# Sorted expert blocks: both ranks from one product, expert numbers read seven at a time, batch 0 joined from block 24

## The reference, cut to what matters

```python
x = x + L0_gnn(layernorm(x), adj)          # 8 batches of 1024 rows, 128 features
x = x + L0_ffn(layernorm(x))               # the part the change touches
x = x + L1_gnn(layernorm(x), adj)
x = x + L1_ffn(layernorm(x))

def L0_ffn(x):                             # 8 experts, the best 2 for each row
    xn = normalised x * gamma + beta
    logits = xn @ Wr + br
    top_vals, top_idx = top_k(logits, 2)
    w = softmax(top_vals)
    y_e = gelu(xn @ W1[e] + b1[e]) @ W2[e] + b2[e]      # 128 -> 256 -> 128
    return sum of the two chosen y_e, weighted with w
```

## Time and profile before

| | before |
|---|---|
| median of 3 runs | 1110.0 us |
| the profiled execution, its own time | 1111.47 us |
| its span in the trace | 1109.7 us |
| mean granted TensorE clock | 0.985 |
| PE busy | 1028.6 us (93%) |
| DVE busy | 687.6 us (62%) |
| ACT busy | 767.0 us (69%) |
| POOL busy | 383.1 us (35%) |

### The profile page before, as it was taken

How to read it: one execution, slowest core, us unless ns; L and a number is a source line. 1 busy time by engine, 2 the same in 40 slices (tenths; PEclk the granted TensorE clock), 3 DMA queues, 4 the chain that set the end, 5 groups by cost and what they waited for, 6 DMA issues and landing times. The chain is left out here.

```text
span 1109.7 us, 20072 instructions
## 1 busy us (share of the span) xinstructions
PE 1028.6 (93%) x6446; PEld 743.4 (67%) x6446; DVE 687.6 (62%) x2171; ACT 767.0 (69%) x1176; POOL 383.1 (35%) x468
## 2 busy tenths in 40 slices
PE   4798789788899998799999999999999999999998
PEld 3466556465476777478888888886466666666667
DVE  5678898768654347388999899762533333333336
ACT  4998899776564555488888888885656556556561
POOL 4123778878573222556565653201000000000000
PEclk9999999999899999899999999999999999999999
DMA  8967987723237664423333322110000000000001
GB/s 301 342 268 270 392 318 277 279 72 124 70 97 249 189 196 140 125 68 86 87 91 90 92 84 73 60 30 1 1 10 10 10 20 10 10 19 11 10 16 33
DMA packets 70730, 128.53 MB, mean 116 GB/s; under 512 B 10094, under 2 KB 36316, under 8 KB 69596
## 3 DMA queue, kind: packets, MB, share of 16 engines
q1 hardware_dynamic: 61852, 109.34, 29.1%
q0 software_dynamic: 8192, 16.79, 5.0%
q10 hardware_dynamic: 576, 1.05, 0.3%
HBM read 76.69 MB, written 50.46 MB: 115 GB/s over the span
## 5 line engine op out<-in xcount | busy, mean ns | idle before, releaser
L2428 PEld LDWEIGHTS eY<-Vo,dGW 128*128 128x128 f32 x1024 | 132.5, 192 | 54.0 <-issue 52.7
L588 POOL DMA_INDIRECT sorted_x<-V,AT_I x128 | 125.2, 978 | 58.7 <-issue 37.2
L2428 PE MATMUL eY<-Vo,dGW 128*128 128x128 f32 x1024 | 134.2, 276 | 0.1
L2598 DVE TENSOR_TENSOR dGW<-H,WBC 128x512 f32<-128x512 f32 x80 | 55.3, 692 | 124.9 <-PE eY L2428 124.8
L2411 PE MATMUL eU<-XTN,V 128*128 128x512 f32 x256 | 131.0, 594 | 0.9 <-PEq L2346 0.9
L777 PE MATMUL O<-Y,HS 128*128 128x512 f32 x256 | 131.4, 634 | 0.0
L2419 PE MATMUL eU<-H,V 128*128 128x512 f32 x256 | 131.1, 594 | 0.0
L2029 POOL DMA_INDIRECT W<-sorted_y,ROW_I x96 | 96.8, 1009 | 70.2 <-PE f_T L2103 50.3
L2507 ACT ACTIVATE H<-eU,bn 128x512 f32<-128x512 f32 x128 | 99.5, 777 | 25.5 <-PE eU L2411 16.2
L2130 PEld LDWEIGHTS f_O<-f_XN,f_PT 128*128 128x128 f32 x896 | 106.8, 192 | 12.8 <-DVE X L2241 10.4
L2130 PE MATMUL f_O<-f_XN,f_PT 128*128 128x128 f32 x896 | 109.8, 276 | 2.7 <-DVE X L2241 2.0
(11 more groups left out here) (328 smaller groups left out, 2074.6 us busy)
## 6 DMA issues: line engine op xcount, KB each, us to landing
XTN<-in_adj SPq DMA_DIRECT2D x64, 512.0 KB, 7.3
masks<-NMW SPq DMA_DIRECT2D x8, 2048.0 KB
f_MK<-masks SPq DMA_DIRECT2D x60, 256.0 KB, 2.8
sorted_y<-zero SPq DMA_DIRECT2D x36, 256.0 KB
NMW<-sorted_x SPq DMA_DIRECT2D x25, 256.0 KB, 2.8
sorted_y<-NMW SPq DMA_DIRECT2D x25, 256.0 KB
X<-in_x SPq DMA_DIRECT2D x8, 512.0 KB, 8.3
out_x<-X SPq DMA_DIRECT2D x16, 256.0 KB, 2.3
```

Source lines behind the costliest of these rows:

```text
L588: g_.indirect_dma_start(sorted_x, bass.IndirectOffsetOnAxis(ap=AT_I[b % 2][:, kt:kt + 1], axis=0), XR[b % 2][:, t * P:(t + 1) * P], None). ...
L2428: i = pe.matmul(Y[q][:, t * P:(t + 1) * P], GW[:, j % 2, t * P:(t + 1) * P], Vo[:, e * P:(e + 1) * P], start=(e == 0 and t == 0), stop=(e ...
L2598: v.tensor_tensor(GW[:, j % 2, :], h2(j), WBC[:, e, q * HALF:(q + 1) * HALF], ALU.mult).then_inc(gw_ready, 1)
```

## The change

It does four things. `rank_wholes` and `take_wholes` go: `used_blocks` now also counts each place's blocks less twice those taken early (`filled[:, 1]`), and one product of two columns gives both ranks, next to the count of blocks below (`rank_blocks`, in step 4). `take_rest` (step 4) then makes the wholes and the parts, with two more small instructions; `list_blocks` and `list_rest` move to step 5 and `list_stores` to step 6. DVE's `expert` reads one number at a time for blocks up to 24 and seven at a time for blocks 25, 32 and 39. POOL's gathers of batch 0 wait for `turned >= 18 + t // 2`. JOIN, NORM and TURN each come three blocks earlier.

```diff
-        TAKEN, TO_READY, UNTIL_READY = 5, 12, 13
+        TAKEN, TO_READY, UNTIL_READY = 5, 10, 11
...
-            JOIN, NORM, TURN, LATE, ROWS_STEP = 27, 38, 40, 17, 2 * E + 1
+            JOIN, NORM, TURN, LATE, ROWS_STEP = 24, 35, 37, 17, 2 * E + 1
...
-                    pool.wait_ge(turned, 18 + t)
+                    pool.wait_ge(turned, 18 + t // 2)
...
-                def rank_wholes():
-                    pe.wait_ge(table_step, TAKEN + 1)
-                    pe.matmul(TB[:, 0:1], before[:, :], ubf[:, :], start=True, stop=True).then_inc(table_step, 1)
-
                 def rank_blocks():
-                    pe.wait_ge(table_step, TAKEN + 3)
-                    pe.matmul(TB[:, 0:1], before[:, :], ubf[:, :], start=True, stop=True)
-                    pe.matmul(TB[:, 1:1 + E], ones[:, :], below[:, :], start=True, stop=True).then_inc(table_step, 1)
+                    pe.wait_ge(table_step, TAKEN + 1)
+                    pe.matmul(TB[:, E:E + 2], before[:, :], ubf[:, :], start=True, stop=True)
+                    pe.matmul(TB[:, 0:E], ones[:, :], below[:, :], start=True, stop=True).then_inc(table_step, 1)
...
                     if k == 4:
-                        rank_wholes()
+                        rank_blocks()
                     if k == 5:
-                        rank_blocks()
-                    if k == 6:
                         list_blocks()
...
-                    v.tensor_copy(ubf[:, :], filled[:, :]).then_inc(table_step, 1)
                     op(v.tensor_tensor, used[:, :], used2[:, 0:1], used2[:, 1:2], ALU.add)
-                    v.tensor_scalar(below[:, :], upto[:, :], used[:, :], None, ALU.mult)
+                    op(v.scalar_tensor_tensor, out=filled[:, 1:2], in0=taken[:, :], scalar=-2.0, in1=used[:, :],
+                       op0=ALU.mult, op1=ALU.add)
+                    v.tensor_copy(ubf[:, :], filled[:, :])
+                    v.tensor_scalar(below[:, :], upto[:, :], used[:, :], None, ALU.mult).then_inc(table_step, 1)
...
-                    v.tensor_copy(ubf[:, :], both[:, :]).then_inc(table_step, 1)
-
-                def take_rest():
-                    dve.wait_ge(table_step, TAKEN + 4)
-                    op(v.tensor_copy, got[:, :], TB[:, 0:1])
-                    op(v.tensor_tensor, pick8[:, :], mine[:, :], TB[:, 1:1 + E], ALU.mult)
+                    op(v.tensor_scalar, places[:, 0:1], places[:, 0:1], float(WHOLES - EARLY), -2.0, ALU.min, ALU.mult)
+                    op(v.tensor_tensor, got[:, :], places[:, 0:1], places[:, 1:2], ALU.add)
+                    op(v.tensor_tensor, pick8[:, :], mine[:, :], TB[:, 0:E], ALU.mult)
...
                 def expert(k):
-                    return dve.value_load(EXPERT[0:1, k:k + 1], min_val=0, max_val=E - 1)
+                    if k < WHOLES:
+                        return dve.value_load(EXPERT[0:1, k:k + 1], min_val=0, max_val=E - 1)
+                    if (k - WHOLES) % 7 == 0:
+                        _, seven = nc.values_load_multi_w_load_instructions(EXPERT[0:1, k:k + 7], engines=[mybir.EngineType.DVE],
+                                                                            min_val=0, max_val=E - 1)
+                        for i in range(7):
+                            experts[k + i] = seven[i]
+                    return experts.pop(k)
...
                     if k == 4:
-                        take_wholes()
+                        take_rest()
                     if k == 5:
-                        take_rest()
+                        list_rest()
                     if k == 6:
-                        list_rest()
-                    if k == 7:
                         list_stores()
```

More of the change, by code:

```diff
@@ L313, in program @@
             pf, ef, used, got, rel = (tile(n, [P, 1]) for n in ("pf", "ef", "used", "got", "rel"))
-            ubf, below = tile("ubf", [P, 1], BF16), tile("below", [P, E], BF16)
+            ubf, below = tile("ubf", [P, 2], BF16), tile("below", [P, E], BF16)
             taken, rest, both = tile("taken", [P, 1]), tile("rest", [P, 2]), tile("both", [P, 1])
+            places = tile("places", [P, 2])
             used2, part_rows, hot2 = tile("used2", [P, 2]), tile("part_rows", [P, 1]), tile("hot2", [P, NR])
-            filled, later, least = tile("filled", [P, 1]), tile("later", [P, 1]), tile("least", [1, 4])
+            filled, later, least = tile("filled", [P, 2]), tile("later", [P, 1]), tile("least", [1, 4])
             within, upto_k = tile("within", [P, 2]), tile("upto_k", [1, 2])
@@ L388, in program @@
             X0_MEANS, X0_ROOT, X0_NORM, X0_TURNED, X0_READ = 1, 3, 5, 7, 9
-            JOIN, NORM, TURN, LATE, ROWS_STEP = 27, 38, 40, 17, 2 * E + 1
+            JOIN, NORM, TURN, LATE, ROWS_STEP = 24, 35, 37, 17, 2 * E + 1
             OTHERS, ROWS_FROM = RING + 1, RING + 1
-            assert HC == 2 and NB == 46 and NT == 8 and ROWS_FROM + E < 18 and WHOLES == 25 and EARLY + 16 - 4 <= 24 < JOIN and RING + E // 2 == EARLY == RING + 4
+            assert HC == 2 and NB == 46 and NT == 8 and ROWS_FROM + E < 18 and WHOLES == 25 and EARLY + 16 - 4 <= 24 <= JOIN and RING + E // 2 == EARLY == RING + 4
             assert JOIN + NT + 1 < NORM and TURN + 3 < NB
@@ L818, in _ @@
                         pe.wait_ge(table_step, 1)
-                        pe.matmul(M[1][:, 0:1], before[:, :], ubf[:, :], start=True, stop=True).then_inc(table_step, 1)
+                        pe.matmul(M[1][:, 0:1], before[:, :], ubf[:, 0:1], start=True, stop=True).then_inc(table_step, 1)
                     if b == LAST and c == 2:
@@ L826, in _ @@
                         route(b - 1, range(4, NT))
-                TB, TC, PL = M[0][:, 0:1 + E], M[1][:, 0:5 * NB + 4], M[1][:, HALF - P:HALF]
+                TB, TC, PL = M[0][:, 0:2 + E], M[1][:, 0:5 * NB + 4], M[1][:, HALF - P:HALF]
                 def turn(k):
@@ L1253, in full_blocks @@
                     op(v.tensor_tensor, full[:, :], got[:, :], rowno[:, :], ALU.is_ge)
-                    v.tensor_copy(ubf[:, :], full[:, :]).then_inc(table_step, 1)
+                    v.tensor_copy(ubf[:, 0:1], full[:, :]).then_inc(table_step, 1)
                 def take_full():
@@ L1277, in used_blocks, with take_rest @@
                     op(v.tensor_scalar, got[:, :], got[:, :], -float(WHOLE - PART), None, ALU.add)
-                    op(v.tensor_tensor, filled[:, :], got[:, :], rowno[:, :], ALU.is_ge)
-                    op(v.tensor_tensor, filled[:, :], filled[:, :], taken[:, :], ALU.subtract)
-                    v.tensor_copy(ubf[:, :], filled[:, :]).then_inc(table_step, 1)
+                    op(v.tensor_tensor, filled[:, 0:1], got[:, :], rowno[:, :], ALU.is_ge)
+                    op(v.tensor_tensor, filled[:, 0:1], filled[:, 0:1], taken[:, :], ALU.subtract)
                     op(v.tensor_tensor, used[:, :], used2[:, 0:1], used2[:, 1:2], ALU.add)
-                    v.tensor_scalar(below[:, :], upto[:, :], used[:, :], None, ALU.mult)
-                def take_wholes():
+                    op(v.scalar_tensor_tensor, out=filled[:, 1:2], in0=taken[:, :], scalar=-2.0, in1=used[:, :],
+                       op0=ALU.mult, op1=ALU.add)
+                    v.tensor_copy(ubf[:, :], filled[:, :])
+                    v.tensor_scalar(below[:, :], upto[:, :], used[:, :], None, ALU.mult).then_inc(table_step, 1)
+                def take_rest():
                     dve.wait_ge(table_step, TAKEN + 2)
-                    op(v.tensor_copy, got[:, :], TB[:, 0:1])
-                    op(v.tensor_scalar, hot[:, EARLY:WHOLES], kth[:, 0:WHOLES - EARLY], got[:, :], filled[:, :], ALU.is_equal, ALU.mult)
+                    op(v.tensor_copy, places[:, :], TB[:, E:E + 2])
+                    op(v.tensor_scalar, hot[:, EARLY:WHOLES], kth[:, 0:WHOLES - EARLY], places[:, 0:1], filled[:, 0:1], ALU.is_equal,
+                       ALU.mult)
                     op(v.tensor_reduce, later[:, :], hot[:, EARLY:WHOLES], AX_X, ALU.add)
@@ L1303, in take_rest @@
                     v.tensor_tensor(hot[:, WHOLES:NB], hot[:, WHOLES:NB], hot2[:, :], ALU.add).then_inc(table_step, 1)
-                    op(v.tensor_scalar, pick8[:, :], TB[:, 1:1 + E], float(PART), -float(SPARE), ALU.mult, ALU.add)
+                    op(v.tensor_scalar, pick8[:, :], TB[:, 0:E], float(PART), -float(SPARE), ALU.mult, ALU.add)
                     v.scalar_tensor_tensor(out=shift8[:, :], in0=order[:, :], scalar=float(SEATS), in1=pick8[:, :],
```

11 lines of the change are left out of this document (5 added, 6 removed).

## The result

| | before | changed |
|---|---|---|
| median, 20 runs each | 1109.51 us | 1111.58 us |
| lowest to highest | 1107.19 to 1112.18 | 1110.39 to 1115.04 |
| time changed / before | | 1.0020, 95% interval 1.0012 to 1.0027 |
| the profiled execution, its own time | 1111.47 us | 1111.38 us |
| its span in the trace | 1109.7 us | 1109.6 us |

The changed kernel takes 2.07 us more, 0.2%. That is small, but the interval leaves no change out.

The account below looks back on a forecast made before the run. PE bounds the loop, waiting in blocks 7 to 15 for loads held behind table TO, and in 256-row blocks for weights DVE copies. A -2.4 plus B +3.2 gives +0.8: 1110.8 us on the median, range 1107.5 to 1113.4.

Parts of the forecast that it names:

- Part B: Blocks of 256 rows, work(24) to work(45): early join and bulk reads together cost +3.2 us, bounds +0.8 to +5.0.
- The table one step earlier: Before block 7: TO ends 2.7 us earlier, PE is 0.7 us behind at work(7), loads of rows come sooner.
- 0.6 us of waits that were to stay: At the load of block 16: PE still waits 0.4 us, plus 0.2 for SP's reads that may be slowed.
- A: Table's part, work(4) to work(24): of 3.7 us lost, 0.7 lost at the table, 0.6 stay: -2.4, bounds -3.0 to -1.5.
- Joining from step 24: First join on DVE: gathers have landed by 400, DVE comes at about 402; waiting on them costs nothing.
- The joins' own waits: Join steps on PE: 0.1 us lost in each of five, 0.6 once behind a 512-row finish; 1.1 in all.
- Seven numbers a read: DVE's reads for blocks 25, 32, 39: 1.5 us each plus register work; PE stalls 1.0, 3.5 and 1.5 us.
- the prediction's own signs: Wrong if bulk read lasts well under 1 us or over 2, no block 32 stop, or SP waits at 12 or 13.
- the norm's wait: In the 256-row blocks: 0.3 us of old waits at the norm go with the new order.
- the cheap read: Rival, chance 0.18: seven numbers cost 0.67 us like three, B is +0.8, time 1107.8 or less, faster.
- The dear read: Rival, chance 0.16: seven numbers take 2.1 us or more, B +5.0, sum +2.6, 1112.6 us; decides from about 2.0.
- The table that buys nothing: Rival, chance 0.06: SP waits at block 12 or 13 for rows POOL sends, A about -0.5, 1112.7 us.

Follow-up runs that it names:

- x3: The kernel before with the bulk reads of seven alone, without the early table or the early join: 1115.09 us, 1.0046 of before.
- x4: The kernel before with the early join alone (join from block 24, gathers less held back): 1110.15 us, 1.0003 of before.
- x6: x5 with the late join again (blocks 27, 38 and 40, gathers one per block): 1105.09 us, 0.9968 of before.
- x10: The changed kernel with the late join again, so early table and reads of seven remain: 1111.32 us against 1109.38, 1.0029 of before.
- x1: The changed kernel with expert numbers read one at a time again; early table and early join stay: 1105.88 us, 0.9966 of before.
- x2: The kernel before with the table one step earlier and nothing else: 1107.27 us, 0.9975 of before.
- x5: The changed kernel with the 21 expert numbers read ahead, three at a time, in block steps 17 to 23: 1104.52 us against 1109.66, 0.9965.
- x7: The changed kernel with three numbers to a read instead of seven, still read where the first is wanted: 1110.51 us, 1.0013 of before.
- x8: x5 with the 21 numbers read ahead seven at a time, in block steps 17, 19 and 21: 1108.25 us, 0.9995 of before.

## Why the prediction was right, and where it wasn't

The forecast, within 0.2% of before at 1110.8 us, held by a hair: 1111.58 us lies in the range, and +2.07 us (+1.3 to +3.0) stands at the edge of what was called the same. The mechanism was the predicted one: the table gains about 3 us, and the bulk reads stop PE at three places and cost more than that. The total is in part luck. Part B, +5.80 us, lies outside its own bounds (+0.8 to +5.0), 2.6 us above the sum; the table gained 0.5 us more than the sum had it, near its best bound; and the medians differ by +2.07 where the loop of the profiles is +2.9.

- **The table one step earlier: right, step by step.** With the 3.55 us added, the trace has `work(5)` at 320.37 (predicted 320.45), `hot` done at 324.68 (324.65), `work(6)` at 325.41 (325.4), `work(7)` at 329.46 (329.4), TO at 326.85 (326.9) and the load of block 16 at 360.01 (360.15). Only the 0.6 us of waits that were to stay did not: A is -2.89 against -2.4. Against the other executions of the same code (x3, x4) it is -1.8 and -2.2, so the 2.4 was as good as the spread allows.
- **Joining from step 24: right.** The waits for gathers cost nothing, and x4, x6 and x10 show that the early join moves the time by nothing measurable. The joins' own waits were 0.6 + 0.15 + 0.15 us, predicted 1.1. Two of the eight joins, not three, meet longer steps of PE (in x1, steps 24 and 25 last 3.72 and 2.87 us).
- **Seven numbers a read: right in kind and place, too small.** The three stops stand at blocks 25, 32 and 39 as predicted, at 1.35, 3.00 and 2.52 us (6.9) instead of 1.0, 3.5 and 1.5 (6.0). The term that was mis-sized is "0.30 + 6 x 0.20 = 1.5 us": it took one duration for all three, while the read takes 2.15, 1.07 and 2.09. By the prediction's own signs, a read of over 2 us counts against it, and two of the three are. Where the read took 1.07 the stop was 0.5 us shorter than predicted, where it took 2.1 it was 0.35 and 1.0 us longer. At block 39 the read explains only some 0.3 of the 1.0: with its register work it is 2.09 + 7 x 0.27 = 4.0 us, where the prediction had 1.5 + 7 x 0.31 = 3.7. The other 0.7 us is cover that the sum put too high there. The 0.31 us a number for register work and hand-over came out at some 0.27: block 39's read ends at 433.0 + 2.09 = 435.1, and the last of its seven register instructions begins at 436.7, 1.6 us for six steps. By the Trainium skill (Runtime: NRT & Kernel Launch, Instruction fetch mechanics), at about 200 ns a register, the reads would have been 1.4 us, an estimate from that figure. The runs, where the table lies in SBUF, have 0.15 to 0.31 us a register, on both sides of it.
- **What was missing altogether: the granted clock.** The sum had no term for what PE does after a stop. It lost 1.45 us at block 32, over half of B's error. The stops add 0.9 us and small shifts 0.15, the joins' waits take 0.2 off, and 0.3 us is a slip of the sum, in the next point. That is the 2.6 us by which B was too small.
- **Subtracted twice: the norm's wait.** The sum takes off all 3.6 us of old waits and then 0.3 more "at the norm". But the nine waits of the earlier trace rows hold that one already, on PE's timeline of before:

```profile
440.25 1.10 PE L860 MATMUL T<-NMW 128*128 128x256 f32 x4 [0.24 <-issue]
```

Without the slip B would have been predicted at +3.5 us.

Of the rivals, the cheap read falls: a read of three is 0.75 us and one of seven at least 1.06, and part B is +5.8. The floor of about 600 ns that the Trainium skill (DMA: Bandwidth & Descriptors, Latency and other measured facts) names for this read is not seen either: single reads take 0.30 at the median. The dear read came near: two of three reads passed 2.0 us, and B passed its +5.0. In the profiles the loop's +2.9 us even passes the +2.6 of that rival; the +2.07 of the medians lies between the forecast's +0.8 and it, and nearer to it. But only part of B's excess is the reads, which the one of 1.07 us held down; the larger part is the clock. The table that buys nothing falls with x2.

## What to carry to other kernels

Moving register reads together does not remove their work: each value keeps some 0.27 us on the queue, and seven of them at one place make one stop that no cover there can take, where single ones hid in part. Read such numbers ahead of need, in steps where the engine that reads has idle time, and in pieces that fit into it: three (1.6 us) fitted into 2.3 us and brought part B 2.1 us under before's and 7.9 under that of sevens in place; seven (3.0 to 3.7 us) did not fit. And price a stop of TensorE at more than its length, since the clock may fall behind it: 1.45 us were lost that way here.

The version to keep by its profile is x5, with 1104.52 us: 5.1 us under before by the medians, 3.9 by the ratio, 2.0 to 5.8 by its interval. In measured time it can't be told from x1, x2 or x6, which all beat both kernels, x1 with the simplest code.

## What the runs showed that was not expected

**The clock behind a stop.** The granted clock fell behind PE's stops of 3.00 us (twice, in the change and its repetition), 3.2 and 2.75 (x3), 2.19 (x7) and 2.85 (x10), with means of 0.55 to 0.74 in the stretch behind; it stayed at 1.00 behind 2.5 (in both again) and behind 3.22 (x10). The same kernel did the same both times, which speaks against chance; the length of the stop alone doesn't decide. What does was not tried and stays open.

**The duration of a bulk read differs by its place, and repeats.** The read of seven from number 32 on takes 1.06 to 1.08 us in all five profiles with sevens, whether it runs ahead of need at 381 us (x8) or in its place at 413 to 416 us; from number 25 on it takes 1.6 to 2.15 and from number 39 on 1.7 to 2.1. Reads of three take 0.75 us from nearly every position (1.00 once), single ones 0.30 at the median. In x8 the three reads run at other times than in the rest and stand in the same order, so the traffic of the moment, which was the guess behind the second rival, doesn't decide it alone. The position in the table may, but in all five profiles the short read is also the second of the three, and the two were not tried apart: the cause stays open.
